# An attention kernel: two fp32r parts for three bf16 parts, heads in pairs on 64-row tiles, and a new order of blocks and loads

## The chip, the cores and the metric

The kernel runs on one core of one Trainium2 chip. The metric is the time of one execution in device microseconds. A core has TensorE (PE) for matrix products, VectorE (DVE), ScalarE (ACT), GpSimd (POOL) and SyncE (SP), each with its own stream of instructions and synchronised by semaphores, SBUF as working memory with 128 partitions, and PSUM with eight banks of 512 fp32 values per partition, into which PE writes. Sixteen DMA engines move data; SP, ACT and POOL issue transfers to them, each in its own queue.

## The reference

One transformer block for 4096 tokens of width 256, 16 heads of 16 values. Attention is causal, with rotary positions; then a residual and a layer norm; then a feed-forward network (256 to 1024 gated, two layers 1024 to 1024 with gelu, back to 256), a residual and a layer norm. All in fp32.

```
q, k, v = heads(x @ Wq.T + bq), heads(x @ Wk.T + bk), heads(x @ Wv.T + bv)
q, k = rope(q), rope(k)
att = softmax(where(causal, q @ k.T / 4, -inf))          # 16 heads, 4096 x 4096
x = layernorm(x + (att @ v) @ Wo.T + bo)
h = silu(x @ w1.T * s1) * (x @ w2.T * s2)
h = gelu(h @ h1.T * hs1); h = gelu(h @ h2.T * hs2)
out = layernorm(x + h @ w3.T * s3)
```

## The kernel before, in words

Four stages run one after the other, each a block of its own: `project` (q, k and v, written to DRAM), `attend`, `widen` (output projection, norm, first half of the network) and `narrow` (the rest). Only `project` and `attend` are touched by the change.

**project** goes over 8 chunks of 512 tokens. Per chunk it makes four units (q and k, two halves of 128 features): two fp32 products on PE (main and rotated), then on VectorE bias and cosine, bias and sine, the sum (L186), and the split into three bf16 parts (L190 to L197). SP stores the parts. Two v products per chunk go beside them.

**attend** works on quads of 4 heads (4 quads), in each on 8 blocks of 512 queries (c), in each on groups of 128 keys (j, 4 per chunk of keys, so 4(c+1) groups in a block, 144 in a quad, 576 in all). Softmax needs the maximum of each query's row before the exponentials, and the kernel makes the scores twice. A *row unit* (L388) has 128 queries on the output partitions and up to 512 keys on the free axis; VectorE takes the maximum over them from PSUM (L477). A *key unit* (L405) has 128 keys on the partitions and up to 512 queries on the free axis; ScalarE takes the exponential (L550). The negated maxima ride as extra contraction rows of the key unit (ones on the key side), so nothing is subtracted. `values` (L418) multiplies a group's four probability tiles with the values: four fp32 matmuls, each into its own 32 partitions of one PSUM bank. Full precision of the scores comes from splitting q and k: six pairs of bf16 parts stacked along the contraction (`TERMS`), 96 rows, and 99 with the maxima. On the diagonal a matmul of a mask with the identity adds -1e30 to the scores (L396, L415).

The path of a block's maxima: VectorE reduces the segments, splits the result in three bf16 parts, PE turns it (L403), VectorE copies it, SP writes it to DRAM and reads it back into the q stack (`store_max`), and only then may the block's key units run. To have it ready, the row units run half a quad ahead: an opening stretch makes the maxima of quad 0's first four blocks (160 row units), and in the body each group gets its even share of the row units of what comes half a quad later (`spread`). Row and key units have rings of three PSUM banks each, the probabilities a ring of three groups. `values` of a group comes one group after its key units. POOL issues the stack loads (30 transfers and the values for a quad) and the stores of the outputs; SP carries only the maxima in this stage. In the last quad the loop repeats its pattern: 160 row units and four maxima are made that nobody needs, and one more quad is loaded.

## Time and profile before

| | |
|---|---|
| median of three runs | 3186.88 us (3184.31 to 3187.11) |
| span of the profiled execution | 3187.4 us (the page gives this as its only time; what lies around it is not listed) |
| PE busy | 2923.3 us, 92% |
| VectorE busy | 2145.0 us, 67% |
| ScalarE busy | 1310.6 us, 41% |
| granted clock, mean | 0.951 |
| project | 0 to about 171 us |
| attend: first row unit, first key unit, end | 238.5, 329.1, about 1966 us |
| widen | about 1974 to 2682 us |
| narrow | 2682 to 3187 us |

A page of the profile lists busy time by engine and by group of instructions; "L477 DVE" is the VectorE instruction of line 477. Matmuls overlap in the pipeline: a duration of 0.38 us does not say that the next one starts 0.38 us later; the distance between two starts is the price in a dense stream.

### The profile page before, as it was taken

Reading aid. Unit: us, or ns where it says so; the run is one execution under the profiler, and the core shown is the slowest. Engines: PE = TensorE matmul, PEld = TensorE weight load, DVE = VectorE, ACT = ScalarE, POOL = GpSimd, SP = SyncE. Lnnn points to the kernel's source line nnn. Section 1 sums busy time; section 2 is a strip of 40 time slices with the busy share of each in tenths; the row PEclk is TensorE's granted clock in tenths of the full one; section 3 lists DMA queues with packets and bytes.
Section 4 is the critical chain, followed back from the end, with each engine's and each line's share of the span. In section 5 each row is a group of like instructions: output and inputs, shape, how many; then the busy total and the mean of one; then the engine's idle time right before and its main releaser. Section 6 shows DMA issues by size and latency. Waiting matters only on the chain. (4 is left out here: it accounts for less than half of the span.)

```text
span 3187.4 us, 51027 instructions
## 1 busy us (share of the span) xinstructions
PE 2923.3 (92%) x15876; PEld 1538.9 (48%) x15876; DVE 2145.0 (67%) x3822; ACT 1310.6 (41%) x2546; POOL 145.8 (5%) x215
## 2 busy tenths in 40 slices
PE   8909999999999999999999997399999995799998
PEld 4402333333333333333333332277777774688887
DVE  7919888888888878888788885655555551434433
ACT  0000677777777766777767764011111110011010
POOL 0070000002000020000200000000000000000000
PEclk9955999999999999999999998699999998899999
DMA  5488000007100062000340001211111003121200
GB/s 158 151 112 99 9 8 5 5 5 81 32 5 5 6 68 45 5 5 6 47 63 8 5 6 64 92 53 53 53 53 53 33 34 127 59 74 39 79 14 20
DMA packets 80648, 146.59 MB, mean 46 GB/s; under 512 B 27452, under 2 KB 50876, under 8 KB 76840
## 3 DMA queue, kind: packets, MB, share of 16 engines
q0 software_dynamic: 11440, 45.43, 10.5%
q1 hardware_dynamic: 60344, 77.47, 7.2%
q10 hardware_dynamic: 8640, 20.85, 2.0%
q8 instruction: 124, 2.03, 0.3%
q14 instruction: 100, 0.82, 0.1%
HBM read 92.67 MB, written 51.04 MB: 45 GB/s over the span
## 5 line engine op out<-in xcount | busy, mean ns | idle before, releaser
L477 DVE TENSOR_REDUCE at_segmax<-at_row 128x1 f32<-128x512 f32 (+3 forms) x2464 | 1414.3, 636 | 315.5 <-PE at_row L393 181.3
L550 ACT ACTIVATE at_probs<-at_key 128x512 f32<-128x512 f32 (+3 forms) x2304 | 1141.9, 566 | 626.6 <-PE at_key L411 349.8
L393 PE MATMUL at_row<-at_k_stack,at_q_stack 96*128 96x512 bf16 (+3 forms) x2464 | 910.4, 378 | 98.5 <-DMA at_k_stack<-k_parts 75.2
L411 PE MATMUL at_key<-at_q_stack,at_k_stack 99*128 99x512 bf16 (+3 forms) x2304 | 831.4, 363 | 4.1 <-issue 1.6
L393 PEld LDWEIGHTS at_row<-at_k_stack,at_q_stack 96*128 96x128 bf16 x2464 | 237.2, 98 | 785.7 <-DVE at_segmax L477 590.9
L428 PE MATMUL at_o<-at_probs,at_values 128*32 128x512 f32 (+3 forms) x4608 | 572.7, 569 | 1.4 <-issue 0.7
L411 PEld LDWEIGHTS at_key<-at_q_stack,at_k_stack 99*128 99x128 bf16 x2304 | 225.8, 98 | 145.9 <-ACT at_probs L550 16.8
L1005 PE MATMUL na_h<-na_h_h,na_h2w_h 128*128 128x512 f32 x512 | 203.3, 397 | 46.2 <-DVE na_h_l L1058 46.2
L1043 ACT ACTIVATE na_h3f<-na_h,na_hs 128x512 f32<-128x512 f32 x64 | 44.0, 688 | 442.6 <-PE na_h L1005 442.6
L739 PE MATMUL wi_f<-wi_h_h,wi_h1w_h 128*128 128x512 f32 x512 | 207.4, 405 | 10.5 <-DVE wi_h_l L870 10.5
L1005 PE MATMUL na_h<-na_h_l,na_h2w_h 128*128 128x512 f32 x512 | 203.2, 397 | 0.0
L1005 PE MATMUL na_h<-na_h_h,na_h2w_l 128*128 128x512 f32 x512 | 203.0, 396 | 0.0
L739 PE MATMUL wi_f<-wi_h_h,wi_h1w_l 128*128 128x512 f32 x512 | 201.3, 393 | 0.0
L739 PE MATMUL wi_f<-wi_h_l,wi_h1w_h 128*128 128x512 f32 x512 | 200.2, 391 | 0.0
L1065 DVE CAST na_h_h<-na_h3f 128x512 fp32r<-128x512 f32 x64 | 27.3, 426 | 252.6 <-ACT na_h3f L1043 252.6
L802 ACT ACTIVATE wi_h<-wi_f,wi_hs 128x512 f32<-128x512 f32 x64 | 44.0, 688 | 342.5 <-PE wi_f L739 342.4
L428 PEld LDWEIGHTS at_o<-at_probs,at_values 128*32 128x32 f32 x4608 | 90.8, 108 | 192.4 <-ACT at_probs L550 158.1
L817 DVE RECIPROCAL wi_recip<-wi_p 128x512 f32<-128x512 f32 x32 | 107.2, 3351 | 57.2 <-PE wi_p L714 57.2
L739 PE MATMUL wi_f<-wi_x1t_h,wi_w_h 128*128 128x512 f32 x256 | 101.8, 398 | 35.2 <-DVE wi_h1w_l L884 35.2
L396 PE MATMUL at_row<-at_ident,at_mask 128*128 128x128 bf16 x576 | 132.1, 230 | 0.0
L1005 PEld LDWEIGHTS na_h<-na_h_h,na_h2w_h 128*128 128x128 f32 x512 | 96.6, 189 | 69.9 <-issue 46.6
L739 PEld LDWEIGHTS wi_f<-wi_h_h,wi_h1w_h 128*128 128x128 f32 x512 | 96.5, 189 | 37.7 <-issue 13.3
(109 smaller groups left out, 2578.6 us busy)
## 6 DMA issues: line engine op xcount, KB each, us to landing
hidden<-wi_h SPq DMA_DIRECT2D x64, 256.0 KB, 2.0
na_h2f<-hidden SPq DMA_DIRECT2D x8, 2048.0 KB, 8.4
at_q_stack<-q_parts POOLq DMA_DIRECT2D x120, 128.0 KB, 25.5
at_k_stack<-k_parts POOLq DMA_DIRECT2D x30, 512.0 KB, 30.6
outputs<-at_outs POOLq DMA_DIRECT2D x32, 256.0 KB, 2.3
wi_o<-outputs SPq DMA_DIRECT2D x8, 1024.0 KB, 5.8
q_parts<-pr_parts SPq DMA_DIRECT2D x48, 128.0 KB, 1.9
k_parts<-pr_parts SPq DMA_DIRECT2D x48, 128.0 KB, 2.2
```

Source lines behind the costliest of these rows:

```text
L393: last = nc.tensor.matmul(bank[:, 0:w], qst[u][0:SROWS, c, h, i * P:(i + 1) * P], kst[u][0:SROWS, h, s * CH:s * CH + w], start=True, stop= ...
L396: last = nc.tensor.matmul(bank[:, w - P:w], mask[:, :], ident[:, :], start=False, stop=True)
L411: last = nc.tensor.matmul(bank[:, q0:CH], kst[u][0:SROWS + PARTS, h, j * P:(j + 1) * P], qst[u][0:SROWS + PARTS, c, h, q0:CH], start=True, ...
L428: last = nc.tensor.matmul(o_ps[32 * h:32 * h + 32, q0:CH], vq[u][:, at:at + 32], probs[:, g % RING_P, h, q0:CH], start=(j == 0), stop=last_j)
L477: nc.vector.tensor_reduce(segmax[:, r, s:s + 1], row_ps[slot][:, 0:w], op=ALU.max, axis=AX.X).then_inc(rows_taken, 1)
L550: nc.scalar.activation(probs[:, g % RING_P, h, q0:CH], key_ps[(QUAD * g + h) % RING_S][:, q0:CH], ACT.Exp).then_inc(probs_ready, 1)
L739: last = nc.tensor.matmul(bank[:, :], w[a][:, k, cols], act_in[b](k), start=(n == 0), stop=(n == 3 * pieces_k - 1))
L802: nc.scalar.activation(h2[:, k % 2, :], fb[k % 4][:, :], ACT.Gelu, scale=hs[:, k:k + 1]).then_inc(hid_taken, 1)
L817: nc.vector.reciprocal(recip[:, q % 2, :], pb[q % 2][:, :]).then_inc(den_taken, 1)
L1005: last = nc.tensor.matmul(hb[k % 4][:, :], h2w[a][:, c, cols], h2[b][:, c, :], start=(m == 0), stop=(m == 3 * FK - 1))
L1043: nc.scalar.activation(h3f[:, k % 2, :], hb[k % 4][:, :], ACT.Gelu, scale=hs[:, k:k + 1]).then_inc(hid_taken, 1)
L1065: nc.vector.tensor_copy(h3[0][:, k, :], h3f[:, k % 2, :]).then_inc(h3_high, 1)
```

## The change

In **project** q and k are split in two fp32r parts instead of three bf16 parts: two of five VectorE operations of the split and sum go, and each unit stores two fp32 parts (2 x 256 KB) for three bf16 ones (3 x 128 KB). GpSimd fills a tile of ones, which SP stores to DRAM.

In **attend** `TERMS` has three pairs, so that a head needs 48 contraction rows, and 50 with the maxima (two parts). Two heads lie in the partitions from 0 and from 64. A row unit does the same 128 queries for both heads, with two matmuls on different 64 rows of the array, into the two banks of one PSUM tile; one VectorE instruction reduces both. Key units stay one head each, at partition 0 or 64. The mask matmuls stay as they are, in bf16 over 128 rows. The rings: two pairs of banks for rows, three banks for keys, one for the output; four groups of probabilities; `values` comes two groups after its key units.

The quads' blocks go up and down in turn (0 to 7, 7 to 0, 0 to 7, 7 to 0). The order of row and key units is written by `interleave`, a small planner with its own costs; all loops are unrolled. The maxima are split on GpSimd, turned by a VectorE transpose of 32x32 blocks three row units later, stored in four transfers and read back in two. The opening stretch, the loop's surplus and the PE turn are gone.

All transfers of the stage are SP's, in this order: ident, mask, first chunk of quad 0's stacks (12 transfers), ones, values, the other seven chunks (12 each), ones, the stacks of quad 1 (12) and its values; then, by the planned order, `store_max` and `store_out` of the blocks; after the last block of quad 0 and of quad 1 the stacks and values of the quad after next. The planned order puts 20 row units ahead of the first key unit, the row units of blocks 1 to 7 end one to two groups ahead of the block's first key group, and each of these blocks begins with 10 or 11 further row units already placed; in the descending quads the lead grows, to 67 row units at block 15; all row units are placed before group 540.

The diff, cut (the waits, declarations and the deletions of old functions are shown in part):

```diff
-PARTS = 3
-TERMS = [(0, 0), (0, 1), (1, 0), (1, 1), (0, 2), (2, 0)]
+PARTS = 2
+TERMS = [(0, 0), (0, 1), (1, 0)]
+RING_R = 2
+RING_K = 3
+RING_P = 4
+VALUE_LAG = 2
...
-                            dve.wait_ge(parts_stored[s], it * 192 + 48 * (2 * u + i) + 48)
+                            dve.wait_ge(parts_stored[s], it * 128 + 32 * (2 * u + i) + 32)
                             nc.vector.tensor_copy(parts[:, s, 0, :], full[:, :]).then_inc(step, 1)
                             dve.wait_ge(step, steps + 2)
-                            nc.vector.tensor_tensor(rest[:, :], full[:, :], parts[:, s, 0, :],
-                                                    ALU.subtract).then_inc(step, 1)
-                            dve.wait_ge(step, steps + 3)
-                            nc.vector.tensor_copy(parts[:, s, 1, :], rest[:, :]).then_inc(parts_ready, 1)
-                            dve.wait_ge(parts_ready, it * 4 * PAIRS + 2 * m + 1)
-                            nc.vector.tensor_tensor(parts[:, s, 2, :], rest[:, :], parts[:, s, 1, :],
+                            nc.vector.tensor_tensor(parts[:, s, 1, :], full[:, :], parts[:, s, 0, :].bitcast(F32),
                                                     ALU.subtract).then_inc(parts_ready, 1)
...
+    blocks = []
+    for quad in range(NQUAD):
+        blocks += [(quad, c) for c in (range(NCH) if quad % 2 == 0 else reversed(range(NCH)))]
+    rows = [(n, i, p, s) for n, (_, c) in enumerate(blocks) for i in range(TPC) for p in range(2) for s in range(c + 1)]
+    groups = [(n, j) for n, (_, c) in enumerate(blocks) for j in range(TPC * (c + 1))]
+    return blocks, rows, groups
...
+    last_row = {n: r for r, (n, _, _, _) in enumerate(rows)}
+    before = []
+    pe = dve = act = 0.0
+    row_end, key_end, max_ready = [], [], {}
+    r = k = 0
+    while k < QUAD * len(groups):
+        n, j = groups[k // QUAD]
+        key_at = key_end[k - RING_K] if k >= RING_K else 0.0
+        row_at = row_end[r - RING_R] if r >= RING_R else 0.0
+        if r <= last_row[n] or (r < len(rows) and row_at <= max(pe, key_at, max_ready[n]) and row_at <= max(key_at, max_ready[n])):
+            m, i, p, s = rows[r]
+            w = row_width(blocks[m][1], i, s)
+            pe = max(pe, row_at) + 0.6 * w + 30.0
+            dve = max(dve, pe + 200.0) + 2 * w * 1.04 + 60.0
+            row_end.append(dve)
+            if r == last_row[m]:
+                max_ready[m] = dve + 9000.0
+            r += 1
+            continue
+        before.append(r)
+        w = min(CH, CH - (j * P - blocks[n][1] * CH))
+        pe = max(pe, key_at, max_ready[n]) + 0.45 * w + 30.0
+        act = max(act, pe + 200.0) + w * 0.833 + 90.0
+        key_end.append(act)
+        if k % QUAD == QUAD - 1:
+            pe += 950.0
+        k += 1
+    return before
...
+            def split(n):
+                half = n % 2
+                pool.wait_ge(negmax_ready, n + 1)
+                if n >= 2:
+                    pool.wait_ge(negrows_ready, n - 1)
+                source = negmax[:, half, :].rearrange("p (b x) -> p b x", b=2)
+                nc.gpsimd.tensor_copy(negparts[:, half, :, 0, :], source).then_inc(high_ready, 1)
+                pool.wait_ge(high_ready, n + 1)
+                nc.gpsimd.tensor_tensor(negparts[:, half, :, 1, :], source, negparts[:, half, :, 0, :].bitcast(F32),
+                                        ALU.subtract).then_inc(negparts_ready, 1)
...
+            def load_stacks(u, quad, t0, t1, loaded):
+                q_v = qp_d.rearrange("a (q p b d) t -> a q b d p t", q=NQUAD, p=2, b=2, d=HD)
+                k_v = kp_d.rearrange("a (q p b d) t -> a q b d p t", q=NQUAD, p=2, b=2, d=HD)
+                for b in range(2):
+                    for r, (qa, ka) in enumerate(TERMS):
+                        part = slice(64 * b + r * HD, 64 * b + (r + 1) * HD)
+                        sp.dma_start(qst[u][part, :, t0:t1].bitcast(F32), q_v[qa, quad, b, :, :, t0:t1]).then_inc(loaded, 16)
+                        sp.dma_start(kst[u][part, :, t0:t1].bitcast(F32), k_v[ka, quad, b, :, :, t0:t1]).then_inc(loaded, 16)
+            def load_values(u, quad):
+                sp.dma_start(vq[u][:, 0:NT * QUAD * VW], v_d[quad].rearrange("p n i e -> p (n i e)")
+                             ).then_inc(values_loaded[quad], 16)
+            def load_ones(u):
+                for b in range(2):
+                    sp.dma_start(kst[u][64 * b + SROWS:64 * b + SROWS + 2, :, :].bitcast(F32), ones_d
+                                 ).then_inc(ones_loaded[u], 16)
+            def store_max(n):
+                u, c = blocks[n][0] % 2, blocks[n][1]
+                sp.wait_ge(negrows_ready, n + 1)
+                for k in range(TPC):
+                    sp.dma_start(max_d[n].rearrange("b a p (i k x) -> (b a p i) k x", k=4, x=32)[:, k, :],
+                                 negrows[32 * k:32 * k + 32, n % 2, :]).then_inc(max_spilled, 16)
+                sp.wait_ge(max_spilled, 64 * (n + 1))
+                if n >= 4:
+                    sp.wait_ge(max_stored[n % 4], 32 * (n // 4))
+                for b in range(2):
+                    sp.dma_start(qst[u][64 * b + SROWS:64 * b + SROWS + 2, :, c * CH:(c + 1) * CH].bitcast(F32), max_d[n, b]
+                                 ).then_inc(max_stored[n % 4], 16)
+            def store_out(n):
+                quad, c = blocks[n]
+                sp.wait_ge(out_taken, n + 1)
+                sp.dma_start(o_d[c, quad, :, :], outs[:, n % 2, :]).then_inc(out_stored[n % 2], 16)
...
+            load_stacks(0, 0, 0, CH, first_loaded[0])
+            load_ones(0)
+            load_values(0, 0)
+            for c in range(1, NCH):
+                load_stacks(0, 0, c * CH, (c + 1) * CH, first_loaded[c])
+            load_ones(1)
+            load_stacks(1, 1, 0, T, stacks_loaded[1])
+            load_values(1, 1)
+            done = 0
+            for g in range(NG):
+                for h in range(QUAD):
+                    for r in range(done, before[QUAD * g + h]):
+                        n = rows[r][0]
+                        if r == last_row[n]:
+                            store_max(n)
+                    done = before[QUAD * g + h]
+                if g in out_after:
+                    store_out(out_after[g])
+                    quad, c = blocks[out_after[g]]
+                    if out_after[g] % NCH == NCH - 1 and quad + 2 < NQUAD:
+                        sp.wait_ge(probs_used, last_group[out_after[g]] + 1)
+                        load_stacks(quad % 2, quad + 2, 0, T, stacks_loaded[quad + 2])
+                        load_values(quad % 2, quad + 2)
...
-            def row_unit(u, c, i, h, s, count, slot):
-                w = CH if s < c else (i + 1) * P
-                bank = row_ps[slot]
-                pe.wait_ge(rows_taken, count + 1)
-                last = nc.tensor.matmul(bank[:, 0:w], qst[u][0:SROWS, c, h, i * P:(i + 1) * P],
-                                        kst[u][0:SROWS, h, s * CH:s * CH + w], start=True, stop=(s < c))
+            def row_unit(r):
+                n, i, p, s = rows[r]
+                quad, c = blocks[n]
+                u = quad % 2
+                w = row_width(c, i, s)
+                q = slice(c * CH + i * P, c * CH + (i + 1) * P)
+                k = slice(s * CH, s * CH + w)
+                bank = row_ps[r % RING_R]
+                if r >= RING_R:
+                    pe.wait_ge(rows_taken, r - RING_R + 1)
+                for b in range(2):
+                    part = slice(64 * b, 64 * b + SROWS)
+                    last = nc.tensor.matmul(bank[:, b, 0:w], qst[u][part, p, q], kst[u][part, p, k],
+                                            start=True, stop=(s < c))
                 if s == c:
-                    last = nc.tensor.matmul(bank[:, w - P:w], mask[:, :], ident[:, :], start=False, stop=True)
+                    for b in range(2):
+                        last = nc.tensor.matmul(bank[:, b, w - P:w], mask[:, :], ident[:, :], start=False, stop=True)
...
+                part = slice(64 * b, 64 * b + SROWS + 2)
+                if m >= RING_K:
+                    pe.wait_ge(probs_ready, m - RING_K + 1)
+                bank = key_ps[m % RING_K]
+                last = nc.tensor.matmul(bank[:, q0:CH], kst[u][part, p, j * P:(j + 1) * P],
+                                        qst[u][part, p, c * CH + q0:(c + 1) * CH], start=True, stop=(j < TPC * c))
...
+            for r, (n, i, p, s) in enumerate(rows):
+                w = row_width(blocks[n][1], i, s)
+                x = p * TPC + i
+                dve.wait_ge(rows_ready, r + 1)
+                nc.vector.tensor_reduce(segmax[:, n % 2, x:x + 2 * TPC + 1:2 * TPC, s], row_ps[r % RING_R][:, :, 0:w],
+                                        op=ALU.max, axis=AX.X).then_inc(rows_taken, 1)
+                if r == last_row[n]:
+                    finish(n)
+                    turn_at[min(r + 3, NR - 1)] = n
+                if r in turn_at:
+                    turn(turn_at[r])
```

## Rows read from the trace of the kernel before

**Rows 1.** Page: busy time, share of the span, instructions of each engine.
```profile
PE 2923.3 (92%) x15876; PEld 1538.9 (48%) x15876; DVE 2145.0 (67%) x3822; ACT 1310.6 (41%) x2546; POOL 145.8 (5%) x215
```
**Rows 2.** Windows: stretch, length, busy (count) of PE, PEld, DVE, ACT, POOL, clock, DMA, GB/s.
```profile
1400.00:1900.00 500.00, 492.77 (x3151) 171.21 (x3150) 415.63 (x773) 353.63 (x713) 21.35 (x40) 1.00 0.15 21
```
**Rows 3.** Groups of attend: shapes, count, busy us, mean ns, idle before and its releaser.
```profile
L477 DVE TENSOR_REDUCE at_segmax<-at_row 128x1 f32<-128x512 f32 (+3 forms) x2464 | 1414.3, 636 | 315.5 <-PE at_row L393 181.3 <-PE at_row L396 127.0
L550 ACT ACTIVATE at_probs<-at_key 128x512 f32<-128x512 f32 (+3 forms) x2304 | 1141.9, 566 | 626.6 <-PE at_key L411 349.8 <-PE at_key L415 269.6
L393 PE MATMUL at_row<-at_k_stack,at_q_stack 96*128 96x512 bf16 (+3 forms) x2464 | 910.4, 378 | 98.5 <-DMA at_k_stack<-k_parts 75.2 <-DVE at_segmax L477 16.2 <-issue 4.2
L428 PE MATMUL at_o<-at_probs,at_values 128*32 128x512 f32 (+3 forms) x4608 | 572.7, 569 | 1.4 <-issue 0.7 <-ACT at_outs L542 0.5
```
**Rows 4.** One tile's instructions (at_key): duration min/median/max ns, first and last start us.
```profile
L411 PE MATMUL at_key<-at_q_stack,at_k_stack x2304: 216/379/634, 329.1 to 1964.6; 99*128 99x512 bf16 x160, 99*128 99x384 bf16 x20, 99*128 99x128 bf16 x12
```
**Rows 5.** Timeline in the dense stretch: start, duration, engine, line, operation.
```profile
700.72 0.38 PE L393 MATMUL at_row<-at_k_stack,at_q_stack 96*128 96x512 bf16 x1
700.93 0.38 PE L411 MATMUL at_key<-at_q_stack,at_k_stack 99*128 99x512 bf16 x1
701.24 1.06 PE L428 MATMUL at_o<-at_probs,at_values 128*32 128x512 f32 x8
702.24 0.28 PE L393 MATMUL at_row<-at_k_stack,at_q_stack 96*128 96x256 bf16 x1
702.36 0.22 PE L396 MATMUL at_row<-at_ident,at_mask 128*128 128x128 bf16 x1
702.42 0.38 PE L393 MATMUL at_row<-at_k_stack,at_q_stack 96*128 96x512 bf16 x1
```
**Rows 6.** Timeline at attend's end: a narrower values group and its follower.
```profile
1963.14 0.85 PE L428 MATMUL at_o<-at_probs,at_values 128*32 128x384 f32 x8
...
1963.92 0.23 PE L411 MATMUL at_key<-at_q_stack,at_k_stack 99*128 99x128 bf16 x1
```
**Rows 7.** Timeline of PE round a turn of maxima (48 weight columns).
```profile
859.31 0.24 PE L403 MATMUL at_turn<-at_ident,at_maxparts 128*48 128x128 bf16 x1
859.48 0.23 PE L393 MATMUL at_row<-at_k_stack,at_q_stack 96*128 96x128 bf16 x1
```
**Rows 8.** Timeline of PE in narrow: fp32r operands, 256 and 512 columns.
```profile
2840.12 0.28 PE L1017 MATMUL na_y<-na_w_l,na_h_h 128*128 128x256 f32 x1
2840.24 0.39 PE L1005 MATMUL na_h<-na_h_h,na_h2w_h 128*128 128x512 f32 x1
2840.47 0.40 PE L1005 MATMUL na_h<-na_h_l,na_h2w_h 128*128 128x512 f32 x1
```
**Rows 9.** Timeline of VectorE in the opening stretch: 15 maxima of 512 back to back.
```profile
279.69 8.78 DVE L477 TENSOR_REDUCE at_segmax<-at_row 128x1 f32<-128x512 f32 x15
```
**Rows 10.** Timeline of project: the split on VectorE, first and last operation.
```profile
77.90 0.69 DVE L192 TENSOR_TENSOR pr_rest<-pr_full,pr_parts 128x512 f32<-128x512 f32 x1
...
79.09 0.69 DVE L197 TENSOR_TENSOR pr_parts<-pr_rest,pr_parts 128x512 bf16<-128x512 f32 x1
```
**Rows 11.** Windows of project's steady part and of the stack loads; columns as in rows 2.
```profile
108.00:146.00 38.00, 35.07 (x96) 17.70 (x95) 36.31 (x64) 0.00 (x0) 0.00 (x0) 1.00 0.54 167
...
192.00:222.00 30.00, 0.00 (x0) 0.00 (x0) 0.00 (x0) 0.00 (x0) 28.79 (x7) 0.50 1.03 105
```
**Rows 12.** Timeline from project's last products to attend's first row unit.
```profile
161.43 1.89 PE L145 MATMUL pr_v<-pr_wv,pr_xt 128*128 128x256 f32 x8
...
170.44 0.75 DVE L202 TENSOR_TENSOR pr_vals<-pr_v,pr_bv 128x256 f32<-128x256 f32 x2
...
175.94 0.37 SPq L362 DMA_DIRECT2D at_ident<-in_ident  x1
...
238.49 0.26 PE L393 MATMUL at_row<-at_k_stack,at_q_stack 96*128 96x128 bf16 x1 [75.17 <-DMA at_k_stack<-k_parts]
```
**Rows 13.** DMA issues: transfer, queue, count, KB each, median us to landing.
```profile
maxima<-at_maxrows SPq DMA_DIRECT2D x36, 12.0 KB, 1.4
```

363 lines of the change are left out of this document (130 added, 233 removed).

## The prediction, made before the changed kernel ran

> **What bounds the kernel now.** I read the page's first table first: PE is busy for 92% of the span, VectorE for 67%, ScalarE for 41% [rows 1]. That is a mean over stages, so the windows come next: in a stretch of 500 us in the middle of attend PE is busy for 493, VectorE for 416, ScalarE for 354, at full clock [rows 2]. The groups say why: the row maxima sat idle for 315 us in all and the exponentials for 627, nearly all of it for PE's scores, while PE's key and value matmuls waited for almost nothing [rows 3]. The key units run from 329.1 us to the stage's end at about 1966 [rows 4, 6]: 1637 us for 576 groups, 2.84 each.
>
> The timeline prices PE's work by distances between starts [rows 5]. A score matmul of 512 columns costs 0.22, a mask 0.06. The four value matmuls, eight records, start 0.31 after the last key unit (0.09 more than 0.22) and give way 1.00 later: 1.09 together. With 384 columns it is 0.78 [rows 6], so 0.22 per 128 columns and a rest of about 0.12: a diagonal group's values average 0.77. Check on the old kernel: 1792 full row units and as many key units at 0.219 make 785; 512 and 512 on the diagonal at 0.21 (320 columns on average, and the mask) 215; values 448 x 1.09 + 128 x 0.77 = 587; 32 turns at 0.17 [rows 7] 5. Sum 1592 against 1637, so 45 us of waits. PE's stream is the bound, and the same sum can be made for the new one.
>
> The base is the profiled span, 3187.4; the page has no other time for that execution, and it lies 0.5 above the median of the runs, so nothing is added.
>
> **Project.** Two of the VectorE operations of a unit go; from the first removed to the last kept one is 77.90 to 79.09, 1.19 us [rows 10], 4.8 per chunk of 19.2. VectorE was the bound (36.3 of 38 us busy), but PE was busy for 35.1 of the same 38 [rows 11] and is late next. So a chunk gives back only PE's idle time, 1.5 to 2.0 us: 13 over the stage. VectorE also ends nearer to PE: it was done 7.9 us after PE's last products (163.3 and 171.2) [rows 12], and will be about 2.4. Together 19 us, and attend's first transfer goes out at 157 instead of 176. The larger stores (4 MB more, 17 against 13) fit: the engines were at 0.54 there [rows 11].
>
> **The start of attend.** The old kernel waited 62 us, from 176 to 238.5, for quad 0's stacks of 6.3 MB [rows 12], and then made rows for 91 us before the first key unit. The new one has its first chunk after some 8 us and starts the row units then. But PE's order has 20 row units and then key unit 0, which waits for block 0's maxima, and their `store_max` stands in SP's queue behind everything that SP loads first: 8 x 12 + 12 stack transfers, ones, both values, 113 in all. The 20 row units last under 20 us; then PE, VectorE and ScalarE stand still. How long is a matter of bytes: two quads of stacks, 12.6 MB, each transfer to 16 partitions. The old loads, of that shape too, kept all engines busy (share 1.03) at 105 GB/s, while project's transfers to 128 partitions moved 167 GB/s at 0.54 [rows 11], some 300 at full share. 12.6 MB at 105 is 120 us; 2.2 MB of values and the ones, at the better rate, 11. On SP's own queue the small stores of the maxima come behind these. 157 + 1 + 131 = 289, and 6 for the journey (the old single store landed in 1.4 [rows 13]; now four stores, a wait, two loads): first key unit at 295, instead of 329. Bounds: 218 if the stacks load at 300 GB/s (then SP's issue, 113 at 0.4 to 0.5 us, sets it), 310 if all bytes go at 105.
>
> The Trainium skill's page "SBUF — State Buffer" (Door 1: The DMA port swizzle) says that DMA speed follows how many of 16 ports the partitions reach; sixteen partitions from 0 reach 4 of them by its table, which would be an estimate of 109 GB/s of its 436. The trace agrees at 105. By that page the larger rows of the fp32 parts don't help.
>
> **PE's stream.**
> - Row units: 1152 pairs. fp32r at 512 columns costs 0.23 a matmul, at 256 columns 0.12 with its weight load [rows 8], so two loads need 0.24. A pair on two halves of the array costs 0.24 if they run side by side, 0.47 if not. That disjoint tiles can is shown by the values: eight fp32 records of 512 in 1.00 us [rows 5]. I take 0.24: 896 full pairs 215, 256 on the diagonal 61, 512 masks 28.
> - Key units: 1792 full at 0.23 alone; where two of different halves stand together in the order (the middle two of a group, mostly) they may overlap, 0.175 on average. I take 0.20: 358. Diagonal: 512 at 0.14 and masks, 100.
> - Values as before, 587. Sum so far 1349.
> - Changes of tile shape. A mask matmul takes all 128 rows and now stands between matmuls of 64, twice per diagonal row pair and twice per diagonal key unit; 2 x 768, less the 128 that values follow anyway, 1408 changes. The trace has changes only of the number of columns: 0.09 into the values, 0.15 out of them (1.00 less four passes of 0.213), and the turn with 48 columns costs 0.17 where its 128 columns need 0.06 [rows 5, 7]. A change of rows is not shown; it is bounded by 0 and 0.15. I take 0.12: 169 us. The planner counts no masks, so nothing is placed to cover this.
> - Waits. VectorE now takes 1024 elements in one instruction. 512 took 0.585 back to back [rows 9]; 512 more at about 0.55 give 1.14 for a pair, some 0.73 on the diagonal, with the rest 1223 in all, 2.28 per full group. ScalarE needs some 0.52 per key unit, 2.06 a group. PE's full group is 2 x 0.24 + 4 x 0.20 + 1.09 = 2.37. Three engines within 15%, two pairs of banks, a fixed order: I take 60 us of waits for the old 45; 0 to 150 is open.
> - Loads behind the blocks. After quad 1's last block SP loads quad 3, 7.4 MB, 67 us; block 19's rows are placed before group 291 and its keys at 312, some 21 groups, 55 us later. Its maxima are 12 us late. After quad 0 there are 31 groups, enough.
>
> The Trainium skill's page "TensorEngine Tiling (Array Packing)" (Key Properties) says that changing the tiling mode, not just the tile, drains TensorE; its modes include 64 rows as well as 32 columns. For changes of columns the trace agrees, at 0.09 to 0.15; for rows no row here shows it. By the page the 169 us are due, without it they are none.
>
> **The sum.** 1349 + 169 + 60 + 12 = 1590. 295 + 1590 = 1885 for attend's end, against 1966: 81 us earlier. widen and narrow are untouched and follow: 3187.4 - 81 = 3106 us. The surplus row units of the old last quad (160 at 0.21, 34 us) are in the old 1637 and gone here.
>
> **Rivals.**
> 1. *The changes of rows cost nothing.* Then 169 us less, and VectorE at 1223 presses on PE's 1349: 20 us more waits, 2957 us. For it: the mask matmul accumulates into banks that PE has just written, and the old stream passed from 96 rows to 128 and back at 0.06 a mask [rows 5]. Against it: those all were whole-array forms.
> 2. *The 64-row tiles don't run side by side* (slower). PE's matmuls then queue at 0.47 a pair: 206 + 15 more for rows, 61 for keys, 3106 + 282 = 3388. It turns from gain to loss when a pair costs 0.31. For it: the trace has side by side only by columns, where the tiles share a moving stream's rows; two fp32r streams and two 0.12 weight loads have to fit in 0.24. Against it: the values show independent tiles.
> 3. *The loads don't hold the maxima back*: large rows load at up to 300 GB/s, or small stores overtake. First key unit at 218, 77 us earlier: 3029. For it: the old maxima landed in 1.4 us. Against it: those were on another queue than the loads.
>
> **How the numbers follow.** Forecast 0.45, with its own range 3040 to 3190 (waits, key price, start); rival 1 0.28; rival 3 0.14; rival 2 0.13. The range 2930 to 3215 holds the first three and a mild form of rival 2. About 0.2%, 6 us, is what a measurement can tell from no change: faster 0.85, within it 0.03, slower 0.12.
>
> **What would show it.** Project's VectorE done near 152 and PE dense there. No PE work from about 180 to 295, with the waits on the block maxima and DMA at about 105 GB/s. In a full group the two row matmuls start within 0.12 of each other. On the diagonal a mask and its neighbours 0.12 apart beyond their columns: if they stand at 0.06, rival 1. The rows' reduction near 1.2 us. If VectorE is busy for over 95% of the middle of attend, PE was not the bound and the sum is wrong in kind.

## The result, and the profile after

| | before | after |
|---|---|---|
| median of six runs | 3187.16 us (3184.31 to 3189.24) | 3427.64 us (3405.48 to 3480.70) |
| ratio to before, 95% interval | | 1.0751 [1.0699, 1.0802] |
| span and time of the profiled execution | 3187.4 us | 3453.7 us, 3455.47 us |
| granted clock, mean | 0.951 | 0.861 |
| attend: first row unit, first key unit, end | 238.5, 329.1, about 1966 | 167.7, 283.8, about 2238 |
| from attend's end to the end | 1221 us | 1216 us |

The change makes the kernel 7.5% slower; 3106 us was forecast, and the range ended at 3215. (Runs more than 1.5% above the fastest of their kernel, one of the six here, two of ten in e6 and two of four in e10, are in the medians but not in the ratios.) The stages behind attend take what they took, and project and the start went as predicted, the start 11 us early. All of the loss is inside attend, from the first key unit on: 1952 us where 1590 were forecast and 1637 taken before.

The first lines of the page after are the busy times, to be held against [rows 1], and the granted clock in 40 slices of 86 us, in tenths:

```profile
PE 3141.3 (91%) x15616; PEld 1740.3 (50%) x15616; DVE 1932.8 (56%) x2294; ACT 1326.4 (38%) x2545; POOL 32.1 (1%) x91
PEclk9955699999896675988899897559999999799999
```

The line to read is the second. Attend is the slices from the fourth to the 26th; the clock falls to 7, 6 or 5 there again and again, while PE's own line stands at 9. The same line of the page before:

```profile
PEclk9955999999999999999999998699999998899999
```

PE's share of the span is the same as before (91 and 92%), and so says nothing of this: a busy microsecond at 1.2 GHz counts like one at 2.4. The windows say it. First before, over attend's key units; columns as in [rows 2], the clock third from the end:

```profile
329.00:1966.00 1637.00, 1613.64 (x10271) 559.90 (x10269) 1364.26 (x2496) 1156.32 (x2337) 66.25 (x124) 1.00 0.13 20
```

Then after: the idle start, one window at half clock, one at full clock, the whole stretch:

```profile
200.00:260.00 60.00, 0.00 (x0) 0.00 (x0) 0.00 (x0) 0.00 (x0) 0.00 (x0) 0.50 0.99 120
1150.00:1175.00 25.00, 25.00 (x100) 9.29 (x104) 10.11 (x15) 10.77 (x20) 0.42 (x2) 0.50 0.01 2
1625.00:1650.00 25.00, 24.67 (x157) 9.88 (x156) 21.82 (x20) 19.45 (x39) 0.00 (x0) 1.00 0.00 1
284.00:2236.00 1952.00, 1899.42 (x10156) 772.40 (x10160) 1255.48 (x1194) 1171.91 (x2335) 12.94 (x62) 0.82 0.08 13
```

In the second row PE is busy for 25.00 of 25 us and ScalarE gets 20 exponentials; in the third PE is busy for no more and ScalarE gets 39. PE is busy for 99% of the stretch before and for 97% after, but its mean clock fell from 1.00 to 0.82.

**What the clock costs.** In 77 windows of 25 us from 300 to 2225 the mean clock is 0.827: 34.5% of the time, 664 us, at 1.2 GHz. The 34 windows at 0.99 or 1.00 hold 36.7 exponentials each, the 12 at 0.50 hold 22.3. 664 x (1 - 22.3/36.7) = 260 us. That is rough, since the windows differ in what stands in them. The six runs give a second figure: their mean clocks go from 0.849 (3480.70 us) to 0.878 (3405.48), about 2660 us per unit of clock over all six and 2970 over the five without the longest, so that 0.861 to 0.952, before's clock, is 242 to 270 us. Together, these estimates put some 240 to 270 of the 362 us above the forecast on the clock. The time follows the clock from run to run, and this kernel's runs spread over 2.2%, before's over 0.15%.

**The rest, 90 to 120 us, shows at full clock.** Timeline of PE in a full group, as [rows 5]: start, duration, engine, line; L465 key units, L446 row pairs, L484 values, L450 masks (the last three lines from elsewhere in attend):

```profile
844.83 0.49 PE L465 MATMUL at_key<-at_q_stack,at_k_stack 50*128 50x512 f32 x1
844.84 0.73 PE L446 MATMUL at_row<-at_k_stack,at_q_stack 48*128 48x512 f32 x2
845.17 0.63 PE L465 MATMUL at_key<-at_q_stack,at_k_stack 50*128 50x512 f32 x2
845.41 0.62 PE L446 MATMUL at_row<-at_k_stack,at_q_stack 48*128 48x512 f32 x2
846.07 0.50 PE L465 MATMUL at_key<-at_q_stack,at_k_stack 50*128 50x512 f32 x1
846.50 1.06 PE L484 MATMUL at_o<-at_probs,at_values 128*32 128x512 f32 x8
847.49 0.50 PE L465 MATMUL at_key<-at_q_stack,at_k_stack 50*128 50x512 f32 x1
...
1105.13 0.28 PE L446 MATMUL at_row<-at_k_stack,at_q_stack 48*128 48x256 f32 x2
1105.34 0.28 PE L450 MATMUL at_row<-at_ident,at_mask 128*128 128x128 bf16 x2
1105.55 0.74 PE L465 MATMUL at_key<-at_q_stack,at_k_stack 50*128 50x512 f32 x2
```

From 844.83 to 847.49 is 2.66 us for a group that was priced at 2.37; before, the commonest distance between the values of two full groups is 2.85. A key unit and a row pair go in 0.34 (844.83 to 845.17; forecast 0.20 + 0.24): the halves do run side by side, on fp32r. What stands together is a key unit and one matmul of the pair; the two of a pair start 0.32 and 0.23 apart.

Two places cost more than was counted. First, the second and third key units and the second row pair take 0.90 (845.17 to 846.07) where 0.64 was counted. The fourth key unit goes into the bank of the first of its group, and so waits for the first one's exponential. ScalarE's exponentials and PE's weight load (PEld) of the fourth key unit, with the wait in brackets:

```profile
845.42 2.06 ACT L562 ACTIVATE at_probs<-at_key 128x512 f32<-128x512 f32 x4 [0.64 <-PE at_key L465]
846.07 0.18 PEld L465 LDWEIGHTS at_key<-at_q_stack,at_k_stack 50*128 50x128 f32 x1 [0.47 <-ACT at_probs L562]
```

From the start of the first key unit to its exponential it is 0.59 (844.83 to 845.42), to the fourth key unit 1.24. That way, 0.43 into the values and 0.99 for them are the whole 2.66. The form is part of it: the 0.59 is 0.48 in e3, a run of the experiments below with three bf16 parts over the whole array (903.48 to 903.96), whose key matmul lasts 0.38 where this one lasts 0.50. Over all key units the median is 0.494 here, 0.492 in run e12 (fp32r, 64 rows), and 0.395 in run e2 (fp32r, 128 rows).

Second, the values come 0.43 behind the fourth key unit (846.07 to 846.50), where 0.31 was counted. In e3, over the whole array, it is 0.31; in e2, also whole but fp32r, mostly 0.32:

```profile
905.00 0.38 PE L465 MATMUL at_key<-at_q_stack,at_k_stack 98*128 98x512 bf16 x1
905.31 1.06 PE L484 MATMUL at_o<-at_probs,at_values 128*32 128x512 f32 x8
```

So each group has one more change from a 64-row form to one of 128 rows, at 0.11 us, some 50 us over the 448 full groups. The forecast's 1408 changes are those of the masks alone.

The waits of the weight loads in all don't measure the first of these. Here are the changed kernel's and e3's, then VectorE's; columns: waiter, releaser, us, times, longest:

```profile
PEld at_key L465 <- ACT at_probs L562: 460.1, 694, 1.7
...
PEld at_key L465 <- ACT at_probs L562: 405.0, 583, 0.9
...
DVE at_segmax L538 <- PE at_row L446: 535.1, 497, 87.8
```

They are much alike, though e3's key units take 1658 us in all, and the changed kernel's 1952. Many of them are the load ahead of a group's first key unit, 0.84 each, while PE still works on the values, and cost nothing. VectorE waits for PE as it did before, and is not the bound.

```profile
L538 DVE TENSOR_REDUCE at_segmax<-at_row 128x2 f32<-128x1024 f32 (+3 forms) x1152 | 1264.0, 1133 | 657.5 <-PE at_row L446 535.1
L465 PE MATMUL at_key<-at_q_stack,at_k_stack 50*128 50x512 f32 (+3 forms) x2304 | 928.1, 500 | 113.0 <-DMA at_q_stack<-maxima 85.2
```

### The profile page after: what moved, and what is told of

Same layout as the page of the kernel before. It is cut to its first block and busy times, and to the rows that moved or that the text cites. A ratio compares the mean times of both kernels' runs of the same rounds, so it can differ in the third digit from the quotient of the medians.

```text
span 3453.7 us, 39202 instructions
## 1 busy us (share of the span) xinstructions
PE 3141.3 (91%) x15616; PEld 1740.3 (50%) x15616; DVE 1932.8 (56%) x2294; ACT 1326.4 (38%) x2545; POOL 32.1 (1%) x91
## 5 line engine op out<-in xcount | busy, mean ns | idle before, releaser
L538 DVE TENSOR_REDUCE at_segmax<-at_row 128x2 f32<-128x1024 f32 (+3 forms) x1152 | 1264.0, 1133 | 657.5 <-PE at_row L446 535.1
L562 ACT ACTIVATE at_probs<-at_key 128x512 f32<-128x512 f32 (+3 forms) x2304 | 1156.5, 566 | 903.0 <-PE at_key L465 473.1
L465 PE MATMUL at_key<-at_q_stack,at_k_stack 50*128 50x512 f32 (+3 forms) x2304 | 928.1, 500 | 113.0 <-DMA at_q_stack<-maxima 85.2
L465 PEld LDWEIGHTS at_key<-at_q_stack,at_k_stack 50*128 50x128 f32 x2304 | 415.7, 213 | 738.5 <-ACT at_probs L562 460.1
L446 PE MATMUL at_row<-at_k_stack,at_q_stack 48*128 48x512 f32 (+3 forms) x2304 | 632.9, 482 | 56.1 <-DVE at_segmax L538 28.2
L484 PE MATMUL at_o<-at_probs,at_values 128*32 128x512 f32 (+2 forms) x4608 | 673.9, 663 | 0.0
L446 PEld LDWEIGHTS at_row<-at_k_stack,at_q_stack 48*128 48x128 f32 x2304 | 305.2, 215 | 226.7 <-DVE at_segmax L538 123.2
L484 PEld LDWEIGHTS at_o<-at_probs,at_values 128*32 128x32 f32 x4608 | 97.3, 116 | 144.1 <-ACT at_probs L562 87.6
L468 PE MATMUL at_key<-at_mask,at_ident 128*128 128x128 bf16 x512 | 129.3, 253 | 0.0
```

The costliest lines, as they stand in the source:

```text
L446: last = nc.tensor.matmul(bank[:, b, 0:w], qst[u][part, p, q], kst[u][part, p, k], start=True, stop=(s < c))
L465: last = nc.tensor.matmul(bank[:, q0:CH], kst[u][part, p, j * P:(j + 1) * P], qst[u][part, p, c * CH + q0:(c + 1) * CH], start=True, stop= ...
L468: last = nc.tensor.matmul(bank[:, q0:q0 + P], ident[:, :], mask[:, :], start=False, stop=True)
L484: last = nc.tensor.matmul(o_ps[32 * h:32 * h + 32, q0:CH], vq[u][:, at:at + 32], probs[:, g % RING_P, h, q0:CH], start=(j == 0), stop=(g = ...
L538: nc.vector.tensor_reduce(segmax[:, n % 2, x:x + 2 * TPC + 1:2 * TPC, s], row_ps[r % RING_R][:, :, 0:w], op=ALU.max, axis=AX.X).then_inc(r ...
L562: nc.scalar.activation(probs[:, g % RING_P, h, q0:CH], key_ps[m % RING_K][:, q0:CH], ACT.Exp).then_inc(probs_ready, 1)
```

## The experiments

All ratios are to the kernel before, with 95% intervals. "Attend" is the stretch from the first to the last key unit. It and the clock, a mean over the whole kernel, are of the profiled execution.

| run | median us | ratio | clock | attend |
|---|---|---|---|---|
| e1_before48 | 4748.02 | 1.4899 [1.4875, 1.4924] | 0.632 | 331 to 3522 |
| e9_before64 | 4748.53 | 1.4901 [1.4876, 1.4926] | 0.631 | 331 to 3523 |
| e5_before72 | 3214.93 | 1.0092 [1.0075, 1.0109] | 0.943 | 329 to 1983 |
| e2_whole | 3314.52 | 1.0402 [1.0385, 1.0420] | 0.952 | 299 to 2095 |
| e12_tile64 | 3300.97 | 1.0365 [1.0325, 1.0404] | 0.923 | 301 to 2076 |
| e13_scaleonly | 3433.25 | 1.0785 [1.0753, 1.0817] | 0.867 | 283 to 2214 |
| e3_bf16stacks | 3172.39 | 0.9956 [0.9939, 0.9973] | 0.946 | 296 to 1954 |
| e6_nomask | 3164.41 | 0.9922 [0.9897, 0.9947] | 0.906 | 282 to 1929 |
| e14_bf16nomask | 3133.93 | 0.9837 [0.9818, 0.9856] | 0.944 | 297 to 1915 |
| e4_laterquad1 | 3392.12 | 1.0668 [1.0625, 1.0711] | 0.879 | 215 to 2165 |
| e7_valuesfirst | 3500.46 | 1.1016 [1.0955, 1.1076] | 0.862 | 283 to 2261 |
| e10_pairs | 3578.62 | 1.1125 [1.1062, 1.1188] | 0.841 | 283 to 2397 |
| e8_best | 3105.84 | 0.9748 [0.9732, 0.9764] | 0.958 | 210 to 1884 |
| e11_planner | 3131.25 | 0.9816 [0.9800, 0.9833] | 0.952 | 220 to 1916 |

### Is it the tile form? The old kernel over 48, 64 and 72 rows

```diff
-qst[u][0:SROWS, ...], kst[u][0:SROWS, ...]           # row units, 96 rows
-kst[u][0:SROWS + PARTS, ...]                         # key units, 99 rows
+qst[u][0:48, ...], kst[u][0:48, ...]                 # e1: 48; e9: 64; e5: 72, both units
-ACT.Exp
+ACT.Exp, scale=0.001
```

> The kernel before, with one edit: row and key units contract only 48 of the stack's rows (partitions 0 to 47, bf16), so that they are 64-row forms; half of the terms and the maxima are left out, and the exponential has a scale of 0.001 so that it stays finite. Everything else as before. Theory R (the granted clock falls because the scores' matmuls use only half of the array's rows, whatever the type): attend's clock, 0.99 in the kernel before, falls to 0.9 or lower in stretches at 0.5, and the time rises from 3187 to 3250 or more. Theory F (it falls because of fp32r operands): clock stays at 0.99. Theory S (it falls because of stalls round the changes of tile shape): the clock falls here too, since masks and scores alternate, but only where there are diagonal units. At full clock the stage would cost 0.12 us for each change of rows, at most 2 x 1024 more, some 200 us less what is hidden; if such a change is free, 3187.

> The kernel before with row and key units contracting 64 rows: a full 64-row tile, every row of it with data. Left out as in the runs with 48 and 72. With 48 rows the clock was 0.50 through attend, with 72 (whole-array form) 0.94 on the mean, with 96 and 99 it is 1.00. Theory R1 (the form decides): clock 0.50 in attend and a time near 4750, as with 48. Theory R2 (the number of rows decides, the form doesn't): something between, clock 0.6 to 0.95 and 3300 to 4300.

> The kernel before with row and key units contracting 72 of the stack's rows instead of 48 (first run of this kind): a whole-array form again, a quarter less rows than before. Some terms and the maxima are left out, exponential scaled by 0.001. It tells the form from the number of rows. Theory R1 (what counts is the form: a 64-row tile): clock 0.99 in attend, time within 10 us of 3186. Theory R2 (what counts is how many rows carry data): clock between 0.5 and 0.9 in attend, time between 3300 and 4700.

A window of 1000 us in the middle of attend, over 48 rows, then one of 100 us over 64 rows:

```profile
1000.00:2000.00 1000.00, 997.04 (x3232) 227.00 (x3231) 468.44 (x772) 409.40 (x736) 38.38 (x72) 0.50 0.14 18
```

```profile
1000.00:1100.00 100.00, 100.00 (x309) 22.37 (x306) 47.75 (x79) 42.64 (x72) 0.00 (x0) 0.50 0.00 1
```

These kernels leave out part of the products and the maxima, so that their outputs are not the reference's, and their exponentials take 0.001 of the scores. Otherwise they have the order, the bf16 parts, the masks and the buffers of before, and only fewer rows in a matmul. PE is busy for practically all of the stretch, and the clock is 0.50 from its beginning to its end; attend takes twice as long. 48 and 64 rows agree to 0.01%, and 72 rows, where the matmul is a whole-array form again, with the same scale, cost 0.9%, at a clock of 0.98 in attend. So the clock falls without any fp32r, and nearly all of the step lies between 64 and 72 rows, where the form changes. The 28 us that e5 loses fit neither of its two expectations, and stay unexplained. This is the strongest evidence of the study, and it needed nothing of the change but its number of rows.

One thing these runs don't give: they use one half of the array only. No run has bf16 on both halves, so why the clock is 0.50 here and 0.82 in the changed kernel is not shown.

### The same question on the new kernel

```diff
-part = slice(64 * b, 64 * b + SROWS)          # row units; key units: SROWS + 2
+part = slice(0, P)                            # e2, both; e12: slice(64 * b, 64 * b + 64)
...
+nc.gpsimd.memset(x[:, :, :].bitcast(F32), 0.0).then_inc(zeroed, 1)     # two stacks; VectorE the other two
...
-ACT.Exp
+ACT.Exp, scale=0.001
```

The stacks are filled with zeros ahead of the loads. e13 has the scale alone, as control.

> The changed kernel, with row and key units over all 128 partitions instead of 48 or 50 of one half (so both heads' rows are summed; the outputs are not the reference's; unused rows hold zeros; exponential scaled by 0.001). fp32r, order, rings, loads stay. The two matmuls of a pair can't run side by side, and there is no change of rows. First key unit some 20 us later (filling with zeros). Theory R: clock at 0.98 or more from 400 us on; a full group is 4 x 0.23 + 4 x 0.23 + 1.09 = 2.95 us, attend ends near 310 + 448 x 2.95 + 128 x 2.4 + 60 = 2000, time about 3215, below the changed kernel's 3428 though the array does each pair one after the other. Theory F: clock near 0.83 as in the changed kernel, time 3600 or more. Theory S: clock full, as for R.

> The run over 128 rows (3315 us, clock 0.952) with one edit: the contraction is over the 64 rows of one head's half again (zeros in the unused ones), so that the form is a 64-row tile; filling with zeros, order and loads are the same. Theory (form): clock as low as the changed kernel's, 0.85 to 0.88, and a time of 3420 to 3480 though a pair can run side by side. Rival (number of rows named in the instruction, 64 for 48 and 50): clock over 0.92 and time below 3300.

> The changed kernel with the exponential scaled by 0.001 and nothing else (probabilities near 1, outputs not the reference's). Control for the runs over 64 and 128 rows, which had that scale. If the number of rows named made the tiled kernel faster (3301 with 64), this one is like the changed kernel: 3400 to 3480, clock 0.85 to 0.88. If the data did, it is near 3290, clock 0.92.

The stretch of the key units, in e2, e12 and e13:

```profile
298.00:2095.00 1797.00, 1767.49 (x10144) 933.70 (x10145) 1253.16 (x1194) 1176.46 (x2331) 12.95 (x62) 0.99 0.08 14
```

```profile
300.00:2076.00 1776.00, 1712.19 (x10146) 707.96 (x10146) 1252.90 (x1194) 1165.98 (x2333) 13.03 (x62) 0.94 0.09 14
```

```profile
282.00:2213.00 1931.00, 1877.26 (x10144) 764.54 (x10144) 1254.02 (x1194) 1171.18 (x2332) 13.03 (x62) 0.83 0.08 13
```

Over the whole array no two matmuls of scores can lie side by side, and the kernel is still 113 us faster than the changed one. Its clock stays at 0.99, and the masks change no form. It is 100 us slower than was expected of it; a full group takes 3.04 us mostly, for 2.95, which is some 40 us of them. The control shows that neither the scaled scores nor the data they make matter (0.83 for 0.82). e12 was a surprise: the same two halves, but all 64 rows of each named, with zeros in the unused ones, gave 0.94 and 132 us less than the control: what its expectation has as the rival. So the form alone does not fix the clock; the number of rows named counts too. In the old kernel 48 and 64 rows made no difference. How the two combine stays open.

The end of attend shows the form by itself, since all row units are done there and PE has only key units and values. First the changed kernel, then e2:

```profile
2120.00:2200.00 80.00, 76.16 (x262) 24.50 (x258) 0.00 (x0) 37.70 (x78) 0.00 (x0) 0.50 0.02 7
```

```profile
2020.00:2090.00 70.00, 64.88 (x388) 26.90 (x387) 0.00 (x0) 51.04 (x114) 0.00 (x0) 1.00 0.02 8
```

With the same kind of work left, and PE busy for 95% and 93%, the one is at half clock and the other at full clock.

### Three bf16 parts in the new order

```diff
-PARTS = 2
-TERMS = [(0, 0), (0, 1), (1, 0)]
+PARTS = 3
+TERMS = [(0, 0), (0, 1), (1, 0), (1, 1), (0, 2), (2, 0)]
...
-qst = [sb(f"q_stack{u}", [P, 2, T], F32R) for u in range(2)]
+qst = [sb(f"q_stack{u}", [P, QUAD, T], BF16) for u in range(2)]
...
-part = slice(64 * b, 64 * b + SROWS)
+part = slice(0, SROWS)
```

> The changed kernel with one part undone: stacks of three bf16 parts, 96 rows (98 with two bf16 parts of the maxima) over the whole array, project splits in three parts again. Two-bank reductions, order of blocks, planner, rings, transposed maxima, all loads on SP stay. Theory R: clock 0.98 or more; PE's sum is the old one without turns, 1587, and 60 us of waits; project ends 19 us later, so first key unit near 300, attend's end near 1950, time about 3170, a little faster than before. Rival (the order, the rings of two and three, or the chain of the maxima cost the time, not the tiles): clock may be full, but the group stays above 3.0 us and the time above 3300.

```profile
296.00:1954.00 1658.00, 1614.05 (x10147) 546.81 (x10148) 1248.83 (x1194) 1156.30 (x2334) 12.82 (x62) 0.98 0.09 15
...
906.87 0.28 PE L451 MATMUL at_row<-at_ident,at_mask 128*128 128x128 bf16 x2
906.98 0.38 PE L465 MATMUL at_key<-at_q_stack,at_k_stack 98*128 98x512 bf16 x1
```

With the order, the planner, the reduction of two banks and the loads of the change, but matmuls over 96 and 98 rows, the kernel gives 3172.39: 255 us faster than the changed one and 0.44% faster than before. The order, the planner, the reduction and the loads are not what costs; the loss comes with the 64-row tiles and their parts. The two masks take 0.11 here; over 64-row tiles the same two took 0.21 (1105.34 to 1105.55). The matmul behind them is of another type there, and its weight load lasts longer; e2, which is fp32r over the whole array, settles that this is not the reason. Its two masks take 0.10:

```profile
504.73 0.28 PE L454 MATMUL at_row<-at_ident,at_mask 128*128 128x128 bf16 x2
504.83 0.47 PE L469 MATMUL at_key<-at_q_stack,at_k_stack 128*128 128x512 f32 x1
```

Leaving a whole-array form for a 64-row form costs 0.10. The way back costs as much: the least distance from a key unit of 512 columns to its mask is 0.32 in the changed kernel, 0.23 in e2 and 0.21 in e3.

### What the masks cost

```diff
-    if s == c:
-        for b in range(2):
-            last = nc.tensor.matmul(bank[:, b, w - P:w], mask[:, :], ident[:, :], start=False, stop=True)
...
-    if j >= TPC * c:
-        last = nc.tensor.matmul(bank[:, q0:q0 + P], ident[:, :], mask[:, :], start=False, stop=True)
```

These are 1024 matmuls. e6 takes them from the changed kernel, e14 from e3.

> The changed kernel without its 1024 mask matmuls (the causal mask is left out). With them go 1408 changes between 64 rows and 128. If such a change costs 0.12 us at full clock as forecast, 56 + 169 = 225 us of full-clock PE time go, part of it at half clock; the time falls to 3200 or less if the clock stays as it is, and further if the masks' neighbourhood is what brings the clock down (it was low where blocks are short). If changes of rows are free, it falls by the masks' own 60 to 80 us, to about 3350.

> The 3172 us kernel (bf16 stacks over the whole array in the changed kernel's order) without its 1024 mask matmuls. Out of the tiled kernel they took 263 us (3428 to 3164). Theory: here only the matmuls go, 1024 at 0.055 to 0.06, since no shape changes and the clock is full anyway: 3105 to 3120. Rival: the masks cost in the waits of the diagonal groups, whatever the form: 3000 or less.

The same matmuls are worth 263 us with 64-row tiles (3427.64 - 3164.41) and 38 without (3172.39 - 3133.93; 52 to 67 were expected). The difference, 225 us, is what they do by changing the form, against 169 forecast. It holds two things that these runs don't part: the changes themselves, and a better clock, 0.90 in e6's attend for 0.82:

```profile
282.00:1928.00 1646.00, 1552.47 (x9151) 628.24 (x9151) 1245.26 (x1194) 1128.16 (x2331) 13.04 (x62) 0.90 0.09 15
```

By the changed kernel's 2660 us per unit of clock, the rise of the runs' mean clock from 0.867 to 0.899 is 85 us of it; the other 140 are 0.10 for each of 1408 changes, which is the timeline's figure. That is worked out, not isolated; by the steeper slope, 2970, the parts are 95 and 130.

The Trainium skill's page "TensorEngine Tiling (Array Packing)" (Key Properties) has the drain at a change of mode without a price; this case agrees, with the figures above.

### The start

```diff
-load_ones(1); load_stacks(1, 1, 0, T, stacks_loaded[1]); load_values(1, 1)   # SP, before the first store_max
+if rows[r][0] == 3: load_second()                                         # GpSimd, after block 3's split
```

> The changed kernel with quad 1's stacks, ones and values issued by GpSimd after the split of block 3's maxima instead of by SP ahead of block 0's maxima. Theory: SP's queue holds the first key unit back until all bytes have landed (284 us); with half of them gone it comes at about 225, and attend's end and the time fall by 59 us, to about 3370, with the clock as low as before. Rival: the start is made up for later, since VectorE or PE then wait elsewhere: time within 20 us of 3428.

```profile
L476 PE MATMUL at_key<-at_q_stack,at_k_stack x2304: 217/493/794, 214.8 to 2165.0; 50*128 50x512 f32 x160, 50*128 50x384 f32 x20, 50*128 50x128 f32 x6, 50*128 50x256 f32 x6
```

The first key unit is at 214.8 instead of 283.8, and the last at 2165.0 instead of 2234.1: 69 us at both ends, in the two profiled executions. The median moved by 36, and the clock in attend is not the same (0.84 here, 0.82 there), so of the 69 us some 36 to 71 arrive at the end.

The order of SP's queue held the maxima back. In the changed kernel the four small stores of block 0's maxima were issued at 213.67, behind the bulk loads, and the loads that wait for them could go out at 280.92 only:

```profile
213.67 1.82 SPq L387 DMA_DIRECT2D maxima<-at_negrows  x4
280.92 1.39 SPq L393 DMA_DIRECT2D at_q_stack<-maxima  x2
```

In e8 (below) the bulk loads are on GpSimd's queue, and from the same stores to the same loads it takes 7.6 us, though the DMA engines have a share of 1.01 from 190 to 200 us:

```profile
197.53 1.70 SPq L382 DMA_DIRECT2D maxima<-at_negrows  x4
205.16 0.68 SPq L387 DMA_DIRECT2D at_q_stack<-maxima  x1
```

### Two attempts on PE's waits that missed

e7 puts `values` in front of the fourth key unit instead of behind it; e10 lets row pairs go only ahead of every other key unit (`before[k] = before[k - 1]` for odd k).

> The changed kernel with a group's value matmuls issued before its fourth key unit instead of after it, so that the fourth does not wait on the exponential of the first (three banks for keys). In the full-clock stretch of the changed kernel a group costs 2.66 us, 0.3 of it before the fourth key unit. Theory: the group falls to 2.35 to 2.45 at full clock, VectorE becomes the bound at 2.3 to 2.4; 448 x 0.25 = 110 us less where the clock is full, and the clock rises a little because PE has fewer pauses: time 3300 or less. Rival: the wait moves to another unit of the group, time within 30 us of 3428.

> The changed kernel with one edit of its order: row units stand only before even key units, so that the key units of a pair of heads follow each other and can run side by side on their two halves. Theory (half an array working alone is what brings the clock down): more of the stream has both halves at work, the clock rises from 0.86 to 0.9 or more and the time falls below 3350. Rival: the fourth key unit waits more for its bank (three of them), PE pauses more, time 3430 or above.

```profile
702.62 0.49 PE L465 MATMUL at_key<-at_q_stack,at_k_stack 50*128 50x512 f32 x1 [0.22 <-ACT at_probs L562]
702.63 0.72 PE L446 MATMUL at_row<-at_k_stack,at_q_stack 48*128 48x512 f32 x2
703.29 1.07 PE L484 MATMUL at_o<-at_probs,at_values 128*32 128x512 f32 x8
704.28 0.73 PE L465 MATMUL at_key<-at_q_stack,at_k_stack 50*128 50x512 f32 x3
704.63 0.62 PE L446 MATMUL at_row<-at_k_stack,at_q_stack 48*128 48x512 f32 x2
705.46 0.49 PE L465 MATMUL at_key<-at_q_stack,at_k_stack 50*128 50x512 f32 x1 [0.22 <-ACT at_probs L562]
```

The wait for the exponential did not go. Behind the values come the fourth key unit and the next group's first and second (the three at 704.28), and the third then waits for the bank of that fourth one: 0.22 of idle PE, and the group is 2.84 long (702.62 to 705.46). With three key banks and a key matmul of 0.50 the place of `values` only moves it. At equal clock the edit costs little: 3479.92 us at 0.862, for 3455.47 of the changed kernel at 0.861.

e10 was slower by 151 us than the changed kernel. Part of that is clock (0.79 in attend of the profiled execution), but not all: its run at a clock of 0.862 took 3562.60, 107 us more than the changed kernel at 0.861. PE stood idle for 120 of 2114 us in attend, and for 53 of 1952 in the changed kernel. The theory behind e10 was that half an array working alone brings the clock down, so that key units in pairs would raise it. The clock did not rise; with the longer waits in it, the run does not settle the theory either way.

### A version that beats both

```diff
-sp.dma_start(qst[u][part, :, t0:t1], q_v[qa, quad, :, :, t0:t1]).then_inc(loaded, 16)
+pool.dma_start(qst[u][part, :, t0:t1], q_v[qa, quad, :, :, t0:t1]).then_inc(loaded, 16)
...
-negmax = sb("negmax", [P, 2, 2 * 2 * TPC])
-negparts = sb("negparts", [P, 2, 2, 2 * 2 * TPC], BF16)
+negmax = sb("negmax", [P, 2, 32], BF16)
...
-turn_at[min(r + 3, NR - 1)] = n
+turn_at[r] = n
```

This is against e3. GpSimd issues all loads of stacks and values, in the order of use, and SP has only ones, maxima and outputs. The maxima are one bf16 part, written by the reduction and turned at once, for two parts split on GpSimd and turned three row units later.

> The kernel with bf16 stacks over the whole array (3172 us), and three edits: GpSimd issues all loads of stacks and values in the order of their use, so that SP's queue has only maxima and outputs; the maxima are rounded to one bf16 part (what is subtracted from a row's scores need not be exact, the same value goes into sum and numerator), so that the reduction writes it and GpSimd's split goes; the turn follows at once. First key unit from 296 to about 205; attend's end from 1955 to about 1865; time 3172 - 91 = 3080, if VectorE, PE and the loads of later chunks (105 GB/s, 7.5 us a chunk) don't hold the short blocks up. Rival: loads from GpSimd's queue and SP's small transfers share the engines, the maxima come late in the first blocks, and only half is gained: 3130.

> The 3106 us kernel with the planner's costs set to what its own trace shows (row pair 0.86 ns a column, masks counted, key 0.43, values by their width, 7 us for the maxima's way). Its first 400 us of key units had PE at 93 to 97% and clock 0.91 to 0.97. Theory: a closer order gives back 20 to 40 us, 3070 to 3090. Rival: the ring of three key banks sets those gaps, not the order: within 10 us of 3106.

```profile
210.00:1883.00 1673.00, 1611.02 (x10141) 545.41 (x10141) 1252.73 (x1196) 1155.89 (x2331) 35.20 (x70) 0.97 0.13 21
```

3105.84 us: 2.5% faster than before and 9.4% faster than the changed kernel; 3080 was expected, and 3130 by the rival. It keeps of the change the block order, the pairs of banks with one reduction and the planner, and drops the two fp32r parts and the tiles. The first key unit is at 210 instead of e3's 296, and attend is 15 us longer; 67 us less in all. What each of its three edits gives is not parted. e11 gave the planner costs read from the trace and was 25 us slower: its key units start 10 us later and take 22 us more. 20 to 40 us less were expected. The costs read from the trace gave the worse order; why is not shown.

## Why the prediction was wrong

- **Project and the first transfer: right.** 158.5 us against 157; the first row unit at 167.7.
- **The start: right, 11 us early.** PE was idle from 200 to 260 us while the loads moved 120 GB/s at a share of 0.99, where I took 105; first key unit 283.8 against 295. e4 and e8 show that it was the queue: 67 us from the maxima's stores to their loads behind the bulk loads, 7.6 on a queue without them. Rival 3, that the loads don't hold the maxima, is false.
- **Side by side: right.** Rival 2's mechanism, that the tiles queue, is false, though the time fell on its side and beyond its 3388. That the two matmuls of a pair would start within 0.12 of each other did not come: each stands beside a key unit instead, and the price of the stream is as if they did. e2, where the matmuls do queue and no form changes at the masks, took 3315; the forecast's own terms give 3388 - 169 = 3219 for that.
- **Changes of form: right in kind, one kind left out.** 0.10 a change at the masks against 0.12. Rival 1 is false. But the change into the values costs 0.11 more from a 64-row form than the 0.31 that was carried over, 448 times, 50 us, and the sum has nothing for it.
- **Block 19's maxima, 12 us: wrong.** Of PE's waits for maxima of 86.6 us in all, 85.4 are one, the start.
- **Waits, 60 us: too small.** A full group takes 2.66 at full clock and not 2.37, 130 us over 448 of them. 50 of these are the changes into the values; the other 80 are net of what the first units save, and come from the fourth key unit's wait for its bank, where 60 of waits were set for the whole stage. The prediction set this term from the busy times of the engines, and not from the way from a key unit to the end of its exponential, which has three banks to hide in: 1.24 us here. Even with e3's 0.48 for 0.59 it would be 1.13, and with 0.31 and 0.99 behind it 2.43, over the 2.37 (an estimate). Narrow's fp32r matmuls, at 0.39 and 0.40 [rows 8], are over 128 rows, and did not show the 0.50.
- **The step that failed: PE's stream was priced at full clock throughout.** The sum multiplies counts by prices from rows at 1.00 [rows 2, 5] and has no term for the granted clock; no rival has one. It cost some 240 to 270 of the 362 us by which attend missed its forecast, and made the loss: without it the changed kernel would stand at 3175 to 3200 (3427.64 less 2970 or 2660 times 0.952 - 0.867), about where before is. That last figure is worked out, not a run: no kernel with 64-row matmuls held the full clock through attend.

The signs were two. The new kernel leaves more than half of the array's rows empty in a matmul that lasts as long, and no row of the trace before showed a half-height form under load; the prediction gave that form bounds for its cost (0.24 to 0.47 a pair), for its changes (0 to 0.15), and none for the clock that comes with it. And all gains of the change hang on PE, at 97% of its stretch, so that any loss of clock is paid in full.

The Trainium skill's page "TensorE: Matmul & The Clock Gate" (Part 1: The HAM clock gate) ties the lower clock to an engine that has idled and the full one to a busy engine. The idle start agrees with it (200 to 260 us, 0.50). For the half-height forms the traces differ, and the measurement decides: in e1 PE was busy for 997.04 of 1000 us at 0.50.

What is left open: what of the 225 us of the masks is drain and what clock; how the rows named, the form and the use of one half or both share in setting the clock; and some 60 to 90 us of attend, beyond the clock, the values' changes and the longer waits, that I did not place.

## What to carry to other kernels

Ask of every new matmul form not only what it costs at full clock but what clock it is granted, and read the granted clock beside PE's busy share first: PE at 97% with a clock of 0.82 looks like PE at 99% with 1.00. Before packing two small contractions into halves of the array, run the old kernel over the small number of rows: e1 took one edit and shows the danger alone, at its largest. And a queue that carries small, urgent transfers should carry no bulk loads ahead of them; moving one block of loads brought the first key unit forward by 69 us.

## What the runs showed of the hardware that was not expected

- bf16 matmuls of 48 or 64 contraction rows, PE busy throughout: clock 0.50 for 3200 us; of 72 rows: 0.943 over the whole kernel (before: 0.951), 0.98 in attend (before: 1.00).
- fp32r on two 64-row halves: clock in attend 0.82 with 48 and 50 rows named, 0.94 with 64, 0.99 over the whole array with 128.
- Fp32r key units of 50 rows and values alone, PE busy for 95%: clock 0.50; the same over 128 rows, PE busy for 93%: 1.00.
- A change from a 128-row form to a 64-row one: 0.10 us (two masks 0.21 against 0.11 in bf16 and 0.10 in fp32r over the whole array); into the values from a 64-row form 0.43, from a whole-array form 0.31.
- Small stores of maxima on the queue of 12.6 MB of bulk loads: 67 us until the loads that wait for them go out; on a queue of their own, with the engines as busy, 7.6 us.
- A matmul of 512 columns from 50 rows in fp32r lasts 0.50 us, from 98 rows in bf16 0.38, from 128 rows in fp32r 0.40; two halves side by side start within 0.01 us of each other (844.83 and 844.84).
- A kernel whose clock wavers spreads by 2.2% from run to run, one at full clock by 0.1% (e2: 3314.42 to 3316.34).
